# Two mixtures of experts: the last join of the attention inside the first mixture's block, biases added by rows, sums turned without folding, normalisation a group earlier

## What is computed

```python
h = _L0_tok_ref(x, L0_tok_W)                       # tokens, 8 x 1024 x 64
h = jnp.concatenate([h, txt], axis=1)              # 8 x 1056 x 64
h = h + _L0_attn_ref(_layernorm(h), ...)           # softmax attention, 8 heads
h = h + _L0_ffn_ref(_layernorm(h), ...)            # 16 experts, F = 128, top 2, then a normalisation
h = h + _L1_attn_ref(_layernorm(h), ...)           # a recurrence over the tokens
h = h + _L1_ffn_ref(_layernorm(h), ...)            # 8 experts, H = 256, top 2
# a mixture of experts, per token s:
#   c[s, e] = softmax of the two largest gate scores, 0 for the other experts
#   out[s]  = sum_e c[s, e] * (relu(x[s] @ w1[e] + b1[e]) @ w2[e] + b2[e])
# the end of the attention: out = (sum_j p_ij v_j) / (sum_j p_ij), then @ w_out + b_out
```

## Time and profile before

| | us |
|---|---|
| runs of the kernel before, median of 3 | 2081.71 |
| lowest and highest of them | 2078.38, 2097.87 |
| profiled execution | 2085.75 |
| its span, first to last instruction | 2083.9 |
| PE busy | 1835.7 (88%) |
| DVE busy | 1233.1 (59%) |
| ACT busy | 1046.6 (50%) |
| POOL busy | 348.4 (17%) |
| first mixture, 1131 to 1390: PE, DVE, ACT busy of 259.00 | 255.53, 176.83, 132.48 |
| second mixture, 1790 to 2050: PE, DVE, ACT busy of 260.00 | 256.53, 78.69, 133.41 |

### The profile page before, as it was taken

The page is one execution under the profiler, slowest core; times in us unless marked ns, Lnnn a source line. Parts: engine busy times, 40 slices in busy tenths (PEclk is TensorE's granted clock), DMA queues, the critical chain, the costliest instruction groups (busy, mean ns, idle before and its releaser), DMA issues. The chain is left out here.

```text
span 2083.9 us, 41201 instructions
## 1 busy us (share of the span) xinstructions
PE 1835.7 (88%) x15691; PEld 798.1 (38%) x15691; DVE 1233.1 (59%) x3083; ACT 1046.6 (50%) x1967; POOL 348.4 (17%) x330
## 2 busy tenths in 40 slices
PE   6857998989898989899859999998499997999999
PEld 2321222222222222222224444443189884444444
DVE  2448887877786877778514577765536653323321
ACT  1320676767675766667544555544223332555554
POOL 1222000000000000000100246546102343000000
PEclk9975999999998999999989999998769997999999
DMA  5533012111112111201026666440120002332240
GB/s 204 195 73 53 8 29 40 29 40 29 40 28 40 29 40 24 40 13 37 24 56 129 112 130 115 88 86 3 35 56 22 1 2 44 63 78 49 54 83 20
DMA packets 87090, 116.67 MB, mean 56 GB/s; under 512 B 30078, under 2 KB 71128, under 8 KB 84848
## 3 DMA queue, kind: packets, MB, share of 16 engines
q1 hardware_dynamic: 82300, 104.86, 23.9%
q0 software_dynamic: 3104, 8.72, 1.3%
q10 hardware_dynamic: 1492, 0.46, 0.1%
HBM read 95.19 MB, written 18.82 MB: 55 GB/s over the span
## 5 line engine op out<-in xcount | busy, mean ns | idle before, releaser
L795 ACT ACTIVATE b_prob<-b_p_s 128x512 f32<-128x512 f32 x1104 | 571.1, 603 | 347.2 <-PE b_p_s L979 330.6
L818 DVE TENSOR_REDUCE b_m<-b_p_m 128x1 f32<-128x1024 f32 x512 | 603.6, 1219 | 154.2 <-PE b_p_s L979 123.1
L931 PE MATMUL b_p_m<-b_k,b_q 48*64 48x512 bf16 x2048 | 379.3, 425 | 68.7 <-DVE b_m L818 23.2
L979 PE MATMUL b_p_s<-b_q,b_k 51*64 51x512 bf16 x2048 | 362.3, 407 | 8.5 <-ACT b_prob L795 8.0
L1007 PE MATMUL b_p_o<-b_prob,v_all 128*9 128x512 f32 x2304 | 316.4, 633 | 1.0
L931 PEld LDWEIGHTS b_p_m<-b_k,b_q 48*64 48x64 bf16 x2048 | 95.6, 110 | 457.2 <-DVE b_m L818 265.2
L1343 ACT ACTIVATE n_hidden<-n_p_z 128x704 f32<-128x704 f32 x192 | 135.0, 755 | 112.6 <-PE n_p_z L1260 112.6
L1343 ACT ACTIVATE d_hidden<-d_p_z 128x704 f32<-128x704 f32 x192 | 135.0, 755 | 112.0 <-PE d_p_z L1260 112.0
L770 POOL DMA_DIRECT2D sum_scr<-b_sums x48 | 26.3, 548 | 825.1 <-ACT b_sums L785 825.1
L1456 DVE TENSOR_TENSOR d_xg<-d_xd,d_c_wide 128x352 f32<-128x352 f32 x192 | 116.4, 635 | 66.6 <-PE d_p_z L1260 58.4
L1260 PE MATMUL n_p_z<-n_xg,n_w 64*128 64x352 f32 x768 | 142.8, 487 | 0.0
(11 more groups left out here) (332 smaller groups left out, 2151.3 us busy)
## 6 DMA issues: line engine op xcount, KB each, us to landing
d_c_wide<-d_c_scr SPq DMA_DIRECT2D x48, 704.0 KB, 14.2
m_x_all<-n_c_scr SPq DMA_DIRECT2D x48, 352.0 KB, 7.9
xt<-in_x SPq DMA_DIRECT2D x16, 1024.0 KB, 8.6
sum_scr<-b_sums POOLq DMA_DIRECT2D x32, 256.0 KB, 2.7
b_q<-qk_scr SPq DMA_DIRECT2D x96, 66.0 KB
qk_scr<-a_qk_part SPq DMA_DIRECT2D x24, 256.0 KB, 2.8
k_rate<-rate_scr SPq DMA_DIRECT2D x8, 528.0 KB, 4.9
b_k<-qk_scr SPq DMA_DIRECT2D x16, 198.0 KB
```

Source lines behind the costliest of these rows:

```text
L795: nc.scalar.activation(prob[:, U % PR_RING, 0:w], p_s[:, U % S_RING, 0:w], ACT.Exp, scale=float(D) ** -0.5).then_inc(exp_done, 1)
L818: nc.vector.tensor_reduce(m3[:, x, 0:1], p_m[:, s, :, :].rearrange("p k n -> p (k n)"), axis=AX.X, op=ALU.max).then_inc(rows_free, 1)
L931: last = nc.tensor.matmul(out[e:e + 64, k, :], q_st[s][r, i, t * P + e:t * P + e + 64], k_st[s][r, i, k * WIDE:k * WIDE + WIDE], start=Tru ...
L979: last = nc.tensor.matmul(out[e:e + 64, :], k_st[s][r, q, jt * P + e:jt * P + e + 64], q_st[s][r, q, a * WIDE:a * WIDE + WIDE], start=True ...
```

## The change

- **Last join.** The steps of the division and the join (`load_sums`, `spread_inverse`, `invert`, `divide`, `project`, `add_rows`) become functions that both blocks call. For sample 7 they run in the first mixture: SP issues the two loads of sums before the `c_wide` of chunks 1 and 2 and the inverse behind them; DVE inverts in group 2; POOL divides before its first `rstd_of`; PE projects and DVE adds in group 7 (`JOIN_GROUP`). POOL clears the stale semaphores only after that join.
- **Biases by rows.** L1272, `c_rows` and its load go. `weigh_biases` does one matmul of `cT` (all 8 full tiles of a sample at once, 128 or 64 rows) with `b2` laid out as a block diagonal of 512 columns, and a small one for the text rows; `add_biases` adds both to the rows. It runs in group 5 for sample 0, and in group `FIRST_GROUP + 10` for the others. `b2` needs zeros (POOL, `clear_biases`) and 8 small loads in place of one, so that `w_in` waits for 14 loads and not 8.
- **Plain turns.** `turn_out` becomes nine transposes of 128 columns (`fold2` goes); `add_out` adds the two halves one after the other, in four and in two DVE instructions.
- **A group sooner.** `measure`, `gather`, `normalise` and `double` move to the offsets -4, -3, -2 and -2.
- **In the attention**, `keep_weights` comes behind the normalisation of the samples 0 and 1, and POOL computes their `rstd` two sums earlier.

The core of the diff:

```diff
+    BIAS_GROUP = [5] + [first + 10 for first in FIRST_GROUP[1:]]
+    INVERT_GROUP, JOIN_GROUP = 2, 7
...
+            sp.wait_ge(set_up, 1)
+            for t in range(FULL):
+                sp.dma_start(b2[t * E:t * E + E, t, :], b2_arg).then_inc(w_in, 16)
...
             nc.gpsimd.memset(own["yT"][:, SEQ:NT * P], 0.0).then_inc(set_up, 1)
+            if feed:
+                divide = own["late"][3]
+                divide(pool, B - 1)
             for it in range(B):
+                if feed and it == 1:
+                    pool.wait_ge(misc_free, join_use() + 1)
+                    for sem in stale:
+                        pool.sem_clear(sem)
...
+        def weigh_biases(b):
+            pe.wait_ge(misc_free, bias_use(b))
+            pe.wait_ge(kept, 2 * b + 2)
+            nc.tensor.matmul(own["p_g"][:, 0:FULL * D], cT[:, :], b2[:, :, :].rearrange("r t d -> r (t d)"), start=True, stop=True)
+            nc.tensor.matmul(own["p_l"][0:TXT, 0:D], cT_text[:, :], b2[0:E, 0, :], start=True, stop=True).then_inc(misc_full, 1)
...
-                last = nc.tensor.matmul(own["p_g"][:, t % 5 * D:t % 5 * D + D], own["yT"][:, t * P:t * P + P], fold2[:, :], start=True, stop=True)
+                bank, k = (own["p_l"], 0) if t == 4 else (own["p_g"], t % 5)
+                last = nc.tensor.transpose(bank[:, k * P:k * P + P], own["yT"][:, t * P:t * P + P], g.eye[:])
...
-                    pe.wait_ge(c_rows_in[b % 2], 16 * (b // 2 + 1))
-                    nc.tensor.matmul(own["p_y"][0:D, 0:CH], b2[:, :], own["c_rows"][b % 2][:, a * CH:a * CH + CH], start=True, stop=False,
-                                     skip_group_check=True)
...
+        def add_biases(b):
+            dve.wait_ge(misc_full, bias_use(b) + 1)
+            dve.wait_ge(doubled, b + 1)
+            rows = acc[:, b, 0:FULL, :]
+            nc.vector.tensor_tensor(rows, rows, own["p_g"][:, 0:FULL * D].rearrange("p (t d) -> p t d", d=D), ALU.add).then_inc(bias_added, 1)
+            nc.vector.tensor_tensor(acc[0:TXT, b, FULL, :], acc[0:TXT, b, FULL, :], own["p_l"][0:TXT, 0:D], ALU.add).then_inc(bias_added, 1)
...
+            for q in range(2):
+                if q == 1:
+                    dve.wait_ge(half_added, 3 * b + 2 + r)
+                for k, (rows, bank) in enumerate(parts):
+                    n = rows.shape[1]
+                    add = nc.vector.tensor_tensor(rows, rows, bank[:, 0:n * P].rearrange("p (t q d) -> p t q d", q=2, d=D)[:, :, q, :], ALU.add)
...
                 if feed:
+                    load_sums, spread_inverse = own["late"][0:2]
+                    load_sums(sp, B - 1)
                 spread_in(0, chunks)
+                if feed:
+                    spread_inverse(sp, B - 1)
                 run()
...
                 measure(0)
                 gather(0)
-                keep_weights()
                 normalise(0)
                 double(0)
                 measure(1)
                 gather(1)
                 normalise(1)
+                keep_weights()
```

More of the change, by code:

```diff
@@ L597, in attend_stage @@
         max_row = sb("b_max_row", [ROWS, PARTS, P], BF16)
[L598 to L601, removed]
+        bias = sb("c_bias", [P, D])
         p_m = ps("b_p_m", [P, 2, 2, 512])
@@ L693, in attend_stage @@
         MAX_IN = 16 * (PARTS + 1)
[L695 to L708, removed]
         @block.sync
@@ L942, in rows @@
                 if x == JOIN:
-                    r = slice(j % 2 * D, j % 2 * D + D)
-                    for t in range(FULL):
-                        nc.tensor.matmul(out[:, 0, t * D:t * D + D], attT[r, t * P:t * P + P], w_out[r, :], start=True, stop=True)
-                    last = nc.tensor.matmul(out[0:TXT, 1, 0:D], attT[r, TOK:SEQ], w_out[r, :], start=True, stop=True)
+                    last = project(pe, j, out[:, 0, :], out[:, 1, :])
                 elif x < FULL_ROWS:
@@ L1092, in moe_phase @@
     for b in range(B):
-        order += [(OUT_GROUP[b] + r, 1, "out", b, r) for r in range(2)]
+        order += [(OUT_GROUP[b] + r, 1, "out", b, r) for r in range(2)] + [(BIAS_GROUP[b], 3, "bias", b, 0)]
+    if feed:
+        order.append((JOIN_GROUP, 1, "join", B - 1, 0))
     misc_use = {step[2:]: n for n, step in enumerate(sorted(order))}
@@ L1100, in out_use, with join_use, bias_use, biasing @@
         return misc_use["out", b, r]
+    def join_use():
+        return misc_use["join", B - 1, 0]
+    def bias_use(b):
+        return misc_use["bias", b, 0]
+    def biasing(i):
+        return [b for b in range(B) if BIAS_GROUP[b] == i]
     def gating(i, k):
@@ L1130, in moe_phase @@
         own["c_wide"] = [[place["c_wide"][:, s, :, a * CH:a * CH + CH] for a in range(NC)] for s in range(2)]
-        own["c_rows"], own["xd"] = [place["c_rows"][:, s, :] for s in range(2)], [place["xd"][:, s, :] for s in range(3)]
+        own["xd"] = [place["xd"][:, s, :] for s in range(3)]
     else:
-        own["c_wide"], own["c_rows"], own["xd"] = [[sb("c_wide00", [P, PR, CH])]], [sb("c_rows0", [E, SEQ])], [sb("xd0", [P, NT * P])]
-    LOADS = 4 + 2 + 2
+        own["c_wide"], own["xd"] = [[sb("c_wide00", [P, PR, CH])]], [sb("xd0", [P, NT * P])]
+    LOADS = 4 + 2 + FULL
     def normal(b):
@@ L1470, in main @@
                         scale(i + 1)
+                    if feed and i == INVERT_GROUP:
+                        invert = own["late"][2]
+                        invert(dve, B - 1)
+                    if feed and i == JOIN_GROUP:
+                        join_last()
+                    for b in biasing(i):
+                        add_biases(b)
                     for part, k in enumerate(CHOOSE):
```

179 lines of the change are left out of this document (109 added, 70 removed).

## The result

| | before | after |
|---|---|---|
| median of four runs each, us | 2088.18 | 2031.27 |
| lowest and highest, us | 2078.38, 2097.87 | 2029.41, 2032.64 |
| ratio, 95% interval | | 0.9732 (0.969 to 0.9775) |
| profiled execution, us | 2085.75 | 2032.64 |
| its span, us | 2083.9 | 2030.8 |

A forecast was written before the change was run, and what follows sets the result against it. PE's stream was taken to bound the mixtures. The terms summed to -63.3 us, giving 2022.5 from the profiled 2085.75 and 2018.4 from the median 2081.71; the forecast was 2019, range 2007 to 2036.

The forecast's parts named there:

- Bias matmuls out: Both mixtures: 48 bias matmuls on PE go, each 0.73 us; -35.0 us.
- biases by rows in: Both mixtures: 16 pairs of one 512-column and one small matmul on PE, 1.10 us each; +17.6 us.
- Plain turns: Turning sums in the mixtures: nine transposes take 1.26 us for 2.29, in fourteen samples; -14.4 us.
- A group sooner: Mixtures: PE's twelve waits of 0.69 us for ACT's copy before a prepared sample's first turn go; -8.3 us.
- The last join moved: Change from attention to first mixture: block ends when the last sums land, PE starts about 1075.3, not 1097.81; -22.5 us.
- The projection +2.3, its wait +2.5: First mixture, group 7: nine projection matmuls at 0.25 us each, and PE's wait for the late inverse, between 0 and 10.
- the join waits longer: Rival, first mixture: inverse and its spread copy wait behind 2.8 MB; 5 to 12 us more, 2024 to 2031; chance 0.13.
- Gate tail: Last half sample of the attention: two PE waits totalling 5.9 us and a half clock of 1.6 go; -7.5 us.
- Six more loads: Recurrence's start: six more loads of b2 delay the last load PE waits for; +1.0 us, between 0 and 2.3.
- turns one by one: Rival, sums' turns: transposes do not overlap, each costs its own 0.27 us; +16 us, 2035; chance 0.03.
- DVE late: Rival, groups 4 to 6: stalls of 1 to 2 us in 12 to 14 samples; 2035 to 2045 us; chance 0.08.
- less in the way: Rival: join without a wait, recurrence without delay, bias pair at 1.02, no stall; 7 us less, 2011; chance 0.07.

The follow-up runs named there:

- b2: Changed kernel with biases weighed as before, by a product at the head of each of the 48 sums; 2040.78 us (ratio 0.9783).
- a4: Changed kernel with the attention's last two sums written by SP, which waits for them, instead of POOL; 2028.83 us (ratio 0.9699).
- b4: Changed kernel with the last join back at the attention's end; 2039.71 us (ratio 0.9727).
- c0: Changed kernel again with no edit, for a second trace; 2028.92 us (ratio 0.9697).
- c2: Changed kernel with rstd of sample 2 ahead of the last division, last two sums written by SP, join in group 13; 2019.42 us (ratio 0.964).
- a1: Changed kernel with POOL's rstd of sample 2 ahead of the last division in the first mixture; 2033.92 us (ratio 0.9705).
- b3: Changed kernel with sums turned and folded by products with the stacked identity again, one DVE add per half; 2046.82 us (ratio 0.9765).
- d1: Changed kernel with measure, gather, normalise and double a group later again, three, two and one groups ahead; 2038.46 us (ratio 0.9762).
- d2: Changed kernel with keep_weights ahead of the first normalise again and the two rstd two sums later; 2045.52 us (ratio 0.9801).
- b1: Kernel before the change, run again with no edit for a second trace; 2096.2 us (ratio 1.0008).

## Why the prediction was right, and where it was not

The time fell into the range because the mixtures' terms, the tail and the loads were read rightly, and because errors of the rest partly cancelled. The sum, term by term, in its order:

- *Bias matmuls out, -35.0; biases by rows in, +17.6.* By b2 the pair gives 7.1 in the second mixture, where these terms say 8.7. The 0.73 holds; the pair costs 1.28 and not 1.10 from start to start, above the bound of 1.16. The nearest row, 0.91 for 512 columns, was of products that follow one another in a string. The term should read +20.5.
- *Plain turns, -14.4.* Right: 1.28 for nine, +7.1 and +7.8 without them. The exposed end of the second mixture, from the first of its last nine turns to the end of DVE's last add, took 3.45 us before (2077.24 to 2080.69) and 3.60 after (2023.99 to 2027.59): +0.15, where +0.25 was forecast.
- *A group sooner, -8.3.* The waits are gone as said. DVE was not late: in the steady mixture no wait of PE for DVE is listed, and one of 0.4 us for ACT.
- *The last join moved, -22.5.* The step that failed: "The block now ends when the last sums have landed", with a barrier of 0.4 us. The landing was right; POOL's drain of 3.99 us behind it was left out, though it stood in the trace of before, covered by PE's projection and DVE's add. -18.6 measured; a4 took the 4.0 back. The term also put under one name what b4 separates: 5.5 us of it were POOL's clearing.
- *The projection +2.3, its wait +2.5.* The step with the large miss: 14.5 in place of 4.8. The division was forecast "ready at 1101.1", with PE there at 1099.0; it ended at 1103.1, with PE there at 1100.2 (the gates' turn): 2.9 us of wait by that input, near the 2.2. But the prediction made the chain through `rstd`, `normalise`, ACT's copy end in "PE's next turn ... +0.3". What it overlooked is the bank: the join's product may begin only when ACT has emptied it in `keep_gates`, and in ACT's list this stands behind that copy. The wait was 7.4 us (7.0 in c0). It had no term for the clock either, and took the projection at full clock. At half clock the projection then took 3.95 us from start to start (1107.61 to 1111.56) for c2's 2.15, and the group behind it 5.2 for 2.7: 4.3 more. With the 0.7 ahead of the gates' turn, which b4 does not have, 7.4 + 4.3 + 2.15 + 0.7 is the 14.5. Waits and clock together cost 12.4 us, above the forecast's own bound of 10. Rival "the join waits longer" named 5 to 12 us more and an end at 2024 to 2031; by size it is what happened, but its cause was the inverse behind the large copies, and that alone would have cost 3 (a1).
- *Gate tail, -7.5.* -8.5 against the first trace, -19 against the second, more than the bound of 9. The mechanism was right. That the kernel before stays at half clock for a time that differs from execution to execution, and so loses up to 10 us more, could not be seen in one trace.
- *Six more loads, +1.0.* From the first turn of the recurrence's weights to the fold: 1512.78 to 1515.97 before, 1488.58 to 1492.61 after, +0.84.

The mis-sized terms are +2.9 (pair), +3.9 (drain) and +9.7 (join), 16.5 together; with them put right the gain is 46.8. Between the first traces 53.1 were measured: the stretch at half clock in the recurrence of the kernel before adds 10.4, the tail 1.0, and the changed kernel's later fold takes off 5.0. Against the second trace of before (span 2094.4) the difference is 63.6, this time with 10.3 from its longer tail; and beside c0 the medians are 62.6 apart (2091.55 and 2028.92). That such figures come near the 63.3 is luck: the join and the drain cost 13.6 us more than forecast, and the kernel before lost in each of its two traces some 10 us at half clock that the forecast did not know of. The forecast of 2019 was 12 below the median of 2031. With the terms put right it would have said 2035, 1 us inside the upper end of the range.

The rivals: turns one by one and DVE late are refuted by b3 and by the list of waits; "less in the way" is out, as the join waited; the ring behind ACT's copy did not appear in the steady state, but its like was there once, in groups 6 and 7. Of the signs of being wrong, one appeared, a half clock in the mixture, once, at the join.

## What to carry to other kernels

When work is moved to another place, list for it not its inputs alone but the bank it writes: who empties it, what stands ahead of that on its engine, and who wants the bank next; here the move won 13.1 us in one place and lost 14.5 in the other. With `rstd` taken out of the way it lost 7.9 (a1), and 3.5 in a group where the bank is idle (c2), of which 2.1 are the join's products. Read the queues' rows at a block's end too: an engine's drain that is covered today becomes the end of the block when the cover goes. And before a gain is put down to an edit, compare the stages in which nothing was changed, in two traces of each kernel.

## What the runs showed of the hardware

- At the attention's end POOL's queue took 3.8 to 4.0 us to drain (3987 ns in the changed kernel, b4, d1 and d2; 3823 in a4 and c2, whose POOL had nothing more to do), while SP took 0.47, ACT 0.22 and DVE 0.02 us at most.
- PE's clock, once fallen to 1.2 GHz behind waits of 2.4 and 3.5 to 4.6 us, came back some 3 us after the last wait in one trace and some 30 us after it in two others, with PE busy from there on (d2: 1033 to past 1060). In the recurrence of one trace it fell to half for some 24 us at a dip of PE's work that left it at full in thirteen others. Either was worth some 10 us. The Trainium skill says in TensorE: Matmul & The Clock Gate, "Part 1: The HAM clock gate", that the number of slow products at a start differs between runs of one kernel. The traces agree in that the half clock lasts differently long in runs of one kernel, here in its middle; a kernel's start was not looked at.
- A copy of 33 KB issued behind 2.8 MB of others took 13.4 us to land (1083.02, to the issue that waits for it at 1096.46), where it took 2.5 with the DMA engines mostly idle (1077.38 to 1079.84 in the kernel before; their share from 1075 to 1082 is 0.25).
- Not settled: why the attention's fold comes anywhere between 1016.0 (b2) and 1031.5 us (a1) with the same code up to there. The mean granted clock from 165 to 1015 us was 0.93 in c0 (fold 1018.9), 0.92 in the first traces of before and after (1017.9, 1022.9), 0.91 in b1 and b4 (1025.1, 1031.1) and 0.90 in a1 (1031.5), so the later folds go with a lower clock; what makes it fall there was not tried.
